# Looked-up ids brought to all partitions by the transfers themselves, and identity and mask made between gathers

## What is computed

```
e = jnp.stack([tbl_0[ids[:, 0]], ..., tbl_38[ids[:, 38]]], axis=1)       # (512, 39, 32)
p = e[:, ROW, :]; q = e[:, COL, :]                                       # 741 pairs
z = jnp.einsum('bpc,apc,bpa->bp', p, w, q)
h = jnp.concatenate([z, dense_ctx], axis=1)                              # (512, 757)
h = jnp.maximum(h @ W_top1 + b_top1, 0.0)                                # 512 wide
h = jnp.maximum(h @ W_top2 + b_top2, 0.0)                                # 256 wide
y = h @ W_top3
```

## Time and profile before

| | us |
|---|---|
| median of 3 runs | 199.92 (199.55 to 202.13) |
| the profiled execution, whole | 198.71 |
| its span in the trace | 197.0 |
| PE busy in the span | 184.5 (94%) |
| DVE busy | 144.1 (73%) |
| POOL busy | 135.4 (69%) |
| ACT busy | 42.7 (22%) |

### The profile page before, as it was taken

How to read it: one execution, slowest core, us unless ns; L and a number is a source line. 1 busy time by engine, 2 the same in 40 slices (tenths; PEclk the granted TensorE clock), 3 DMA queues, 4 the chain that set the end, 5 groups by cost and what they waited for, 6 DMA issues and landing times.

```text
span 197.0 us, 3278 instructions
## 1 busy us (share of the span) xinstructions
PE 184.5 (94%) x1320; PEld 64.4 (33%) x1320; DVE 144.1 (73%) x137; ACT 42.7 (22%) x64; POOL 135.4 (69%) x202
## 2 busy tenths in 40 slices
PE   6999988969999999999999999799989976999895
PEld 3534533332222222322322222223322212222782
DVE  4889998965899989976663999589664349747600
ACT  4956941030001100111112100110121111210722
POOL 7988899888888888888888888888922200440000
PEclk9999999999999999999999999999999999999999
DMA  6999940000000100000000000000000000000000
GB/s 166 278 290 419 387 138 15 10 17 12 10 13 10 20 10 12 12 14 13 10 13 14 11 13 10 15 13 15 12 0 3 0 0 0 0 5 0 0 0 0
DMA packets 6688, 9.75 MB, mean 49 GB/s; under 512 B 1977, under 2 KB 4477, under 8 KB 6673
## 3 DMA queue, kind: packets, MB, share of 16 engines
q1 hardware_dynamic: 3696, 8.00, 12.6%
q0 software_dynamic: 2944, 1.51, 4.4%
q10 hardware_dynamic: 32, 0.03, 0.1%
HBM read 9.53 MB, written 0.00 MB: 48 GB/s over the span
## 4 chain that ended last, share of the span: by engine, by line
POOL 55%; PE 32%; issue 7%; DVE 2%; DMA 1%; ACT 1%; DVEq 0%; POOLq 0%
POOL gathered L395 41%; POOL pause L402 13%; PE ps L609 10%; PE ps L623 10%; PE ps L634 6%; PE ps L654 4%; PE ps L646 2%; DVE prod L518 2%; DMA gathered<-tbl,ids_sb 1%; POOL sel L384 1%; PE ps L587 1%; PE ps L663 0%; ACT eT L448 0%; POOL sel L387 0%; ACT z_sb L455 0%
## 5 line engine op out<-in xcount | busy, mean ns | idle before, releaser
L518 DVE TENSOR_TENSOR prod<-ps,eT 128x1024 f32<-128x1024 f32 (+2 forms) x91 | 110.2, 1265 | 36.2 <-PE ps L609 31.6
L395 POOL DMA_INDIRECT gathered<-tbl,ids_sb x92 | 92.3, 1003 | 15.2 <-issue 15.0
L609 PE MATMUL ps<-eT,w_sb 32*128 32x512 f32 (+2 forms) x380 | 70.7, 640 | 4.4 <-DVE prod L518 2.9
L623 PE MATMUL ps<-prod,sel 128*32 128x512 f32 x380 | 51.5, 604 | 0.0
L609 PEld LDWEIGHTS ps<-eT,w_sb 32*128 32x128 f32 (+2 forms) x380 | 22.0, 183 | 52.0 <-issue 25.1
L402 POOL MEMSET pause<- 128x256 f32 x91 | 30.3, 333 | 0.1
L503 DVE TENSOR_SCALAR hot<-ids_half,row_of 125x2048 bf16<-125x2048 f16 x34 | 27.8, 881 | 1.5 <-PE ps L576 0.9
L409 POOL TENSOR_TENSOR tabs<-tabs 128x512 f32<-128x512 f32 x8 | 10.1, 1264 | 25.0 <-ACT tabs L469 25.0
L576 PE MATMUL ps<-hot,lower 125*32 125x512 bf16 x272 | 22.0, 401 | 0.0
L634 PE MATMUL ps<-z_sb,w_sb 128*128 128x512 f32 x40 | 20.4, 624 | 0.7 <-ACT eT L448 0.7
L623 PEld LDWEIGHTS ps<-prod,sel 128*32 128x32 f32 x380 | 8.1, 108 | 33.7 <-issue 21.0
(11 more groups left out here) (36 smaller groups left out, 63.5 us busy)
## 6 DMA issues: line engine op xcount, KB each, us to landing
w_sb<-w SPq DMA_DIRECT2D x1, 1536.0 KB
gathered<-tbl,ids_sb POOLq DMA_INDIRECT x92, 2.3
tabs<-hot SPq DMA_DIRECT2D x3, 448.0 KB
w_sb<-wst SPq DMA_DIRECT2D x1, 640.0 KB, 13.1
w_sb<-wst SPq DMA_DIRECT2D x1, 576.0 KB, 12.0
tabs<-hot SPq DMA_DIRECT2D x1, 560.0 KB
w_sb<-wst SPq DMA_DIRECT2D x1, 512.0 KB, 10.5
w_sb<-w SPq DMA_DIRECT2D x1, 512.0 KB
```

The lines of the kernel that those rows point to most:

```text
L395: pool.indirect_dma_start(gathered[J][:, b, K * r:K * r + K], None, tables[f], bass.IndirectOffsetOnAxis(ap=ids_sb[:, F * b + f:F * b + f ...
L518: dve.tensor_tensor(prod[:, x:x + n, :], ps[:, s:s + n, :], eT[:, I:I + 1, :].broadcast_to([P, n, B]), ALU.mult).then_inc(multiplied, 1)
L609: mm = pe.matmul(ps[:, RUN_BANK[p] + i - first, :], w_sb[rows, w_tile(q), :], eT[rows, J, :], start=True, stop=True)
L623: mm = pe.matmul(z_ps[K * (u % G):K * (u % G) + K, :], sel[:, u // G, :], prod[:, RUN_SLOT[p] + t - FIRST_TILE[p], :], start=(u < G), stop ...
```

## The change

The ids of each looked-up block are loaded as 16-bit unsigned halves straight to 125 partitions, by one transfer for each block whose source is one row of 2048 ids (4 KB) read 125 times. The first goes by ACT's queue, the other three by SP's queue, each ahead of the table that follows the one before it. The steps "ids" are gone from the plan, with their products, copies, the `spread` matrix and their waits; `ids_half` is of type uint16 where it was float16. `lower` of block 0 is made in two pieces, and PE waits by piece. The third looked-up block has PSUM banks of its own. The products on zeros become 14 in one row, bfloat16, 128 x 512. POOL makes the identity and the mask not ahead of the gathers but between the first six of them, where the first five fillings of `pause` stood.

```diff
-WARM = [2, 2]
+WARM = 14
+LOWER_PIECES = [[(0, 4), (4, 8)], [(0, 8)], [(0, 8)], [(0, 10)]]
...
-        hot_ids_sb = sb("hot_ids_sb", [NHOT * G, B], I32)
-        ids16 = sb("ids16", [NHOT * G, B], F16)
-        spread = sb("spread", [NHOT * G, NHOT * G, HP], F16)
-        ids_half = [sb(f"ids_half{h}", [P, G, B], F16) for h in range(NHOT)]
+        ids_half = [sb(f"ids_half{h}", [P, G, B], U16) for h in range(NHOT)]
...
-        look_ps = [[ps[:, bank, :] for bank in banks] for banks in [(0, 1), (2, 3), (0, 1), (6, 7)]]
-        ids_ps = [ps[0:HP, bank:bank + G, :] for bank in (0, 4, 4, 4)]
+        look_ps = [[ps[:, bank, :] for bank in banks] for banks in [(0, 1), (2, 3), (4, 5), (6, 7)]]
...
+            def load_hot_ids(h):
+                sp.dma_start(ids_half[h][0:HP, :, :].rearrange("p f b -> p (f b)"),
+                             hot_ids[h:h + 1, :].broadcast_to([HP, G * B])).then_inc(hot_ids_in[h], 16)
...
-            act.dma_start(hot_ids_sb[:, :], hot_ids).then_inc(hot_ids_in, 16)
-            act.wait_ge(hot_ids_in, 16)
-            act.activation(ids16[:, :], hot_ids_sb[:, :], ACT.Copy).then_inc(ids16_made, 1)
+            act.dma_start(ids_half[0][0:HP, :, :].rearrange("p f b -> p (f b)"),
+                          hot_ids[0:1, :].broadcast_to([HP, G * B])).then_inc(hot_ids_in[0], 16)
...
-                        dve.wait_ge(ids_half_made, halves_of(h))
-                        dve.wait_ge(third_made, 1)
+                        dve.wait_ge(hot_ids_in[h], 16)
```

More of the change, by code:

```diff
@@ L10 @@
 BF16 = mybir.dt.bfloat16
-F16 = mybir.dt.float16
 F32 = mybir.dt.float32
@@ L207, in turns, with lowers_of @@
     return TURNS.index(J) + 1
-def halves_of(h):
-    return h + 2
+def lowers_of(h, c):
+    return 2 * (sum(len(pieces) for pieces in LOWER_PIECES[:h]) + 1 + [a <= c < b for a, b in LOWER_PIECES[h]].index(True))
 def lay_out_weights(w, W_top1):
@@ L286, in dlrm_tower @@
         ids_in = sem("ids_in")
-        hot_ids_in = sem("hot_ids_in")
+        hot_ids_in = [sem(f"hot_ids_in{h}") for h in range(NHOT)]
         tab_in = [sem(f"tab_in{h}") for h in range(NHOT)]
@@ L375, in _ @@
         def _(pool):
[L376 to L379, removed]
             for n in ROW_SETS:
                 pool.iota(row_int[n][:, :], pattern=[[1, n]], base=0, channel_multiplier=n).then_inc(rows_numbered, 1)
[L382 to L388, removed]
             pool.wait_ge(ids_in, 16)
             fields = [(J, r) for J in GATHERED for r in range(FIELDS_IN[J])]
-            pauses = 0
+            gathers = pauses = 0
             for J, r in fields:
@@ L420, in _ @@
             for step in PLAN:
[L421 to L431, removed]
+                if step[0] == "lower":
                     h = step[1]
                     act.wait_ge(tab_in[h], 16 * len(tab_pieces))
-                    for i in range(2):
-                        act.activation(lower[i][h][0:HP, :, :], bytes_of[h][0:HP, :, 1 - i::4], ACT.Copy,
-                                       scale=256.0 if i == 0 else 1.0).then_inc(lower_made, 1)
+                    for a, b in LOWER_PIECES[h]:
+                        for i in range(2):
+                            act.activation(lower[i][h][0:HP, :, K * a:K * b],
+                                           bytes_of[h][0:HP, :, 4 * K * a + 1 - i:4 * K * b:4], ACT.Copy,
+                                           scale=256.0 if i == 0 else 1.0).then_inc(lower_made, 1)
                 elif step[0] == "keep":
@@ L536, in side_free @@
                     pe.wait_ge(*side_used.pop())
[L538 to L541, removed]
             pe.wait_ge(warm_zeroed, 1)
-            keep_warm(2, WARM[0])
-            pe.wait_ge(ids16_made, 1)
-            pe.wait_ge(spread_made, 1)
+            zeros = prod[:, 0, :].bitcast(BF16)
+            for _ in range(WARM):
+                pe.matmul(ps[:, 7, :], zeros[:, 0:P], zeros[:, 0:B], start=True, stop=True)
             for step in PLAN:
[L548 to L558, removed]
-                elif step[0] == "look":
+                if step[0] == "look":
                     h, c0, c1 = step[1:]
@@ L678 @@
     arrays["ids"] = np.ascontiguousarray(a["ids"].reshape(NCHUNK, P, F).transpose(1, 0, 2).reshape(P, -1))
-    arrays["hot_ids"] = np.ascontiguousarray(a["ids"].T[[f for fields in HOT_FIELDS for f in fields]])
+    arrays["hot_ids"] = np.ascontiguousarray(np.ascontiguousarray(a["ids"].T).view(np.uint16)[:, ::2]
+                                             [[f for fields in HOT_FIELDS for f in fields]].reshape(NHOT, -1))
     arrays["dense_t"] = np.ascontiguousarray(a["dense_ctx"].T)
```

53 lines of the change are left out of this document (31 added, 22 removed).

## The result

The changed kernel takes 208.47 us, median of 4 runs (207.19 to 210.27), where the kernel before takes 199.85 (199.55 to 202.13, 4 runs): a ratio of 1.041, 95% interval 1.029 to 1.053. It is slower, by 8.6 us; 1.7 us and no more than 5.3 were forecast. The profiled execution took 209.4, its span is 207.7, 10.7 longer than before. Beside some of the runs further down the kernel before took 201 to 204 us, beside others 236 to 250, with the same program, so each run is compared by its ratio to the kernel before timed beside it.

The account below looks back on a forecast made before the run. Gathers up to the keep of block 8, then PE, were taken to bound the kernel. Look 2 3.0 us later less 1.34 us spare gave 1.7; 199.92 + 1.7 = 201.6 us, range 198.9 to 205.2.

Parts of the forecast that it names:

- Two chains that meet at the keep of block 8; 1.34 us free: Gathers and PE's own work meet at 125.7 us; PE can come 1.34 us later there without cost.
- Five engines for 125 rows: Each 125-row ids transfer runs on five DMA engines, 25 rows of 4 KB on each.
- The ids land at 10.9; look 2 ends 3.0 us later: First ids land at 10.9 us after 48 rows at 0.17; first compare at 11.0, look 2 ends at 31.8, not 28.76.
- my upper price: Upper cost of a 4 KB row on one DMA engine: 0.25 us, where 0.17 was taken.
- that rival: DVE's compare takes twice its step on uint16 input, adding 28 us, near 226; chance 0.03.
- Later blocks do not add to it: Each further ids and table pair, 33 rows or 5.6 us, hides under eight compares of 6.6 us.
- my three signs of being wrong: First compare before 9 us, a wait for a later block's ids, or the chain still running over the gathers.
- The clock: PE idles from its products on zeros, at 6 to 8 us, to the first slice; no clock cost was counted.
- The gathers' row: POOL's first gather stays at 4.0 us, within -0.9 and +0.4, and block 8 lands at 125.7.
- Slow rows: Rival: 4 KB rows at 0.25 us on five engines, ids land at 14.7, end 5.5 us later, 205.4; chance 0.13.
- same: The outcome that the time is neither faster nor slower by over 2%, about 4 us; chance 0.79.

Follow-up runs that it names:

- both repairs: Changed kernel with ids transfers cut into 112 and 13 rows, first looked-up ids on SP's queue, identity and mask ahead of the gathers: 200.0 us, ratio 1.000.
- e13: The kernel before, unedited, profiled once more: 200.71 us.
- e2: Changed kernel with look 2's copy (keep 2) placed ahead of lower 3 in the plan: 207.32 us, ratio 1.037.
- e1: Changed kernel with each transfer of looked-up ids cut into 112 and 13 rows: 205.38 us, ratio 1.024.
- e3: Changed kernel with the last ids' transfer behind the first three weight blocks and table 3 in SP's queue: 206.38 us, ratio 1.030.
- e11: Changed kernel with each block's ids laid out 125 times in memory: three of four times within 0.5% of the changed kernel's 258.44 us, the fourth 250.62.
- e7: First run of the changed kernel with both repairs: ratio 0.985, beside a kernel before of 236.51 us.

## Why the prediction was wrong

- *Two chains that meet at the keep of block 8; 1.34 us free:* right. Of the 10.4 us at the keep of block 3, 9.0 remain behind that keep. With both repairs PE waits for the gather at this keep again (0.23 us). But the 1.34 is one execution's: in e13, the same kernel, PE came to this keep with nothing to spare.
- *Five engines for 125 rows:* right, 130 packets on ACT's queue. The Trainium skill's rule on the number of engines (DMA: Bandwidth & Descriptors, on why a DMA increments its semaphore by 16) is shown for 125 rows here.
- *The ids land at 10.9; look 2 ends 3.0 us later:* right, 10.83 and 3.0, but the way to 10.9 was partly luck. I let table 0 be there by 6, and 15 rows of `ids_half[1]` pass ahead of the last row of `ids_half[0]`. Table 0, which stands ahead of `ids_half[1]` in SP's queue, landed only at 10.97. If that queue keeps its order, about 33 long rows (25 and 8) and not 48 had passed by then. With the 1.9, 0.3 and 0.5 of the forecast that is an estimate of (10.83 - 2.7) / 33 = 0.25 us a row, my upper price. Fewer rows at a higher price gave the same time. The late table 0 cost nothing: PE's first slice waited until 12.22 and PE still caught up with DVE by look 2. DVE ran 28 compares without a wait, and a uint16 input left the compare at 0.84 us a step (23.41 / 28), so that rival falls. This agrees with the Trainium skill (VectorE: DVE Perf Modes, what auto-detection checks).
- *"Later blocks do not add to it":* **this step failed.** I counted only pairs of ids and table, 33 rows against eight compares, and never followed table 3. Ahead of it stand three transfers of ids with 25 rows each on the slow engines, and behind the last of these three weight blocks too: 25 + 24 + 8 = 57 rows for the last pair. SP could issue it only at 14.15 us (at 5.17 before), and it landed at 34.3. Tables 1, 2 and 3 landed 5.8, 7.3 and 10.2 us after the one before; by these counts that is an estimate of 0.18, 0.22 and 0.18 us a row, so the count was missed and not the price. ACT takes its steps in order, and lower 3 stands ahead of keep 2, a wait that was nowhere in the sum. Cost 4.8 us, and the clock's 2.6 behind it. e2 shows ACT's order (the keep of block 3 is 2.9 us earlier without it), e1 the five engines, e3 that whatever is last pays. None of my three signs of being wrong came, since none of them looked at a table.
- *The clock:* not in the sum at all. I said that PE would idle before the first slice, and that is harmless, but not that a later wait of 6 us would cost 2.6 us behind it. A fall near 173 added another 1.65, behind waits that the kernel before has without one; that part is not explained. The Trainium skill (TensorE: Matmul & The Clock Gate, why this matters for your kernels) warns of drops behind idle gaps; the rows show one after 6.2 us and, in e1, behind 2.6.
- *The gathers' row:* taken as no change, within -0.9 and +0.4; it was 2.4 us later at the 80th. The rows of the other queue cost more than the 1.4 us that I allowed (eight at 0.17): the ids took 4.2 us to land instead of 2.2, which is eight at 0.25. And the constants in the gaps are not free beside compares. Hidden here, decisive in e1.
- *Slow rows* was the rival nearest in sign, with another mechanism. What it has in common with the result is the price of the first rows (0.25 by the estimate above), but the ids did not land at 14.7, and that 125 reads of one row cost nothing of their own is shown by e11.

In the chances, same stood at 0.79; the measured time is outside the range by 3.3 us. The term I had, 3.0 us less the 1.34, came true; the error is the 4.8 and 2.6 us that I put at nothing, and the 1.65 near 173.

## What to carry to other kernels

Give a transfer a row count that 16 divides, or cut it so (112 + 13 rows here, where 125 ran on five engines), and look not only at its own landing but at what its queue holds behind it. When a transfer gets later, walk every in-order engine's list for the wait on it, and see what stands behind that wait. Price the clock with each idle stretch of PE: here 2.6 to 6 us without products in the middle of the work cost 1.4 to 2.6 us more. And a margin read from one trace, like the 1.34 us here, can be gone in the next execution of the same kernel.

## What the runs showed of the hardware

- A transfer of 125 rows of 4 KB left 125 + 5 packets, and the compare that needs it began at 10.83 us. Cut into 112 and 13 rows it left 125 + 29, and the compare began at 6.60.
- Constants that POOL makes between gathers cost more when DVE compares run beside them: 0.67 to 0.98 us in e1, where 0.20 to 0.46 was seen for the same ones without compares beside them.
- A 500 KB transfer on ACT's queue made a 78 KB transfer issued at the same time on SP's queue land after 4.2 to 5.0 us instead of 2.0 to 2.2.
- Where the kernel before took 236 to 250 us, PE stood before instructions without a releaser (0.7 us and more at a time) only between 53 and 145 us, while gathers ran, and DVE stood without a known one too. With fillings of 64 elements the time rose to 311 and 315 us, and with 208 to 266, though the 80th gather hardly came earlier there (122.63 with both repairs, 123.36 with 256 in e7; 123.19 in the kernel before, 123.17 with 256). What the engines wait for stays open, and so does whether the spacing of the gathers is the cause.
